# Factorization machine on one core: every load is issued by GpSimd instead of SP

## What is computed

```python
x_reg = x @ W_lin.T + b_lin
emb = x @ factors                                   # factors: 12500 x 16
sum_squared = square(emb.sum(axis=1))
squared_sum = (square(x) @ square(factors)).sum(axis=1)
h = relu(emb @ W1.T + b1)                           # 128
h = relu(h @ W2.T + b2)                             # 64
dnn_out = h @ W3.T + b3
y = x_reg + 0.5 * (sum_squared - squared_sum)[:, None] + dnn_out
y = 0.5 + sigmoid(y) * 5.0
```

## Time and profile before

| | |
|---|---|
| median of 3 runs | 133.75 us |
| the profiled execution | 133.76 us |
| its span, first to last instruction | 132.0 us |
| busy: PE / ACT / DVE / POOL | 81% / 47% / 40% / 12% of the span |
| moved by DMA | 52.36 MB, mean 397 GB/s |
| mean granted TensorE clock | 0.974 |
| chain that ended last | DMA 54%, PE 40%, SP's issues 2% |

### The profile page before, as it was taken

How to read it: one execution, slowest core, us unless ns; L and a number is a source line. 1 busy time by engine, 2 the same in 40 slices (tenths; PEclk the granted TensorE clock), 3 DMA queues, 4 the chain that set the end, 5 groups by cost and what they waited for, 6 DMA issues and landing times.

```text
span 132.0 us, 2607 instructions
## 1 busy us (share of the span) xinstructions
PE 107.0 (81%) x1123; PEld 34.6 (26%) x1123; DVE 52.6 (40%) x51; ACT 61.5 (47%) x52; POOL 15.7 (12%) x48
## 2 busy tenths in 40 slices
PE   6099969429979839749749979999998987989992
PEld 4012222002212112112112233322222112345881
DVE  0391063027036036046045016565351351576571
ACT  4030067029039039049048046868562561465851
POOL 3015000200010200200200110164530000000000
PEclk9999999995999999999977999999999999999999
DMA  3999899989999998998999999899999999999700
GB/s 106 413 531 417 377 477 472 407 387 467 427 387 462 457 427 387 457 437 387 467 457 427 387 457 447 377 432 412 452 407 407 462 415 417 418 404 411 302 26 1
DMA packets 3489, 52.36 MB, mean 397 GB/s; under 512 B 404, under 2 KB 536, under 8 KB 1560
## 3 DMA queue, kind: packets, MB, share of 16 engines
q1 hardware_dynamic: 3480, 52.23, 93.2%
HBM read 52.22 MB, written 0.00 MB: 396 GB/s over the span
## 4 chain that ended last, share of the span: by engine, by line
DMA 54%; PE 40%; SPq 2%; DVE 1%; issue 1%; ACT 1%
DMA xr<-in_x_pairs 43%; PE p_lin L506 34%; DMA xr<-in_x_end 11%; PE p_sq L506 2%; PE p_h L601 2%; SPq L273 1%; PE p_tot L506 1%; PE p_h L632 1%; PE p_tot L614 0%; DVE h L454 0%; DVE h L449 0%; SPq L267 0%; SPq L266 0%; PE p_tot L621 0%; SPq L265 0%
## 5 line engine op out<-in xcount | busy, mean ns | idle before, releaser
L327 ACT ACTIVATE sq<-xr 128x2560 f32<-128x2560 f32 x20 | 45.9, 2333 | 46.8 <-DMA xr<-in_x_pairs 38.8
L427 DVE TENSOR_TENSOR sq<-xr 128x1536 f32<-128x1536 f32 x20 | 34.6, 1761 | 53.7 <-DMA xr<-in_x_pairs 42.9
L506 PE MATMUL p_lin<-xr,wr 128*17 128x512 f32 x320 | 39.9, 638 | 15.6 <-DMA xr<-in_x_pairs 14.4
L506 PE MATMUL p_lin<-sq,wz 128*18 128x512 f32 x320 | 37.7, 592 | 0.0
L506 PEld LDWEIGHTS p_lin<-xr,wr 128*17 128x17 f32 x320 | 9.2, 102 | 44.5 <-issue 38.4
L307 POOL COPY wr<-hd 128x136 f32 (+1 forms) x20 | 9.3, 464 | 75.0 <-PE p_lin L506 75.0
L506 PEld LDWEIGHTS p_lin<-sq,wz 128*18 128x18 f32 x320 | 10.1, 98 | 25.8 <-issue 25.0
L506 PE MATMUL p_lin<-xr,hd 128*17 128x352 f32 (+1 forms) x128 | 10.0, 380 | 1.3 <-DMA xr<-in_x_end 1.3
L437 DVE TENSOR_TENSOR sq<-xr 128x1408 f32<-128x1408 f32 (+3 forms) x6 | 6.6, 1135 | 6.1 <-DMA xr<-in_x_end 6.1
L337 ACT ACTIVATE sq<-xr 128x1408 f32<-128x1408 f32 (+3 forms) x6 | 5.7, 983 | 6.3 <-DMA xr<-in_x_end 6.3
L506 PE MATMUL p_lin<-sq,ws 128*18 128x352 f32 x64 | 6.6, 459 | 0.0
(11 more groups left out here) (52 smaller groups left out, 40.8 us busy)
## 6 DMA issues: line engine op xcount, KB each, us to landing
xr<-in_x_pairs SPq DMA_DIRECT2D x8, 4096.0 KB, 21.9
xr<-in_x_groups SPq DMA_DIRECT2D x4, 2048.0 KB, 18.3
xr<-in_x_end SPq DMA_DIRECT2D x1, 2112.0 KB, 10.5
xr<-in_x_end SPq DMA_DIRECT2D x3, 640.0 KB, 12.0
xr<-in_x_end SPq DMA_DIRECT2D x1, 1760.0 KB, 14.3
xr<-in_x_end SPq DMA_DIRECT2D x1, 1056.0 KB, 12.4
hd<-in_head SPq DMA_DIRECT2D x1, 952.0 KB, 4.8
xr<-in_x_end SPq DMA_DIRECT2D x1, 704.0 KB, 13.7
```

Of the source, the lines that this page charges most:

```text
L327: nc.scalar.activation(sq[:, ring(s), BY_DVE:CHUNKS, :], xr[:, s, BY_DVE:CHUNKS, :], ACT.Square).then_inc(act_squared, 1)
L427: nc.vector.tensor_tensor(sq[:, ring(s), 0:BY_DVE, :], xr[:, s, 0:BY_DVE, :], xr[:, s, 0:BY_DVE, :], ALU.mult).then_inc(dve_squared, 1)
L506: return nc.tensor.matmul(out, lhsT, rhs, start=False, stop=False, skip_group_check=True)
```

## The change

All loads move from SP to GpSimd. SP keeps only the three stores of y. GpSimd issues head, x_first, x_rest and pairs 0 to 2 first, then zeroes the pads, and from then on its loads and its copies stand in one program, in the order of the `sq_used` counts that they wait for; of a load and a copy with the same count the load comes first. The hardware loop over 12 groups is written out. The copy of the end weights (`ws`, 32 columns) goes behind the copies for groups 0 to 2. The wait of an end piece loses END_SLOT: pieces 0 and 1 now wait for a count of 19 (before 21), pieces 2 and 3 for 20 (22), the others for 21 (23). Nothing changes on the other engines.

```diff
         @block.sync
         def _(sp):
-            sp.dma_start(hd[:, :], head).then_inc(hd_landed, 16)
-            sp.dma_start(xf[:, :], x_first).then_inc(first_landed, 16)
-            sp.dma_start(xl[:, :, :].rearrange("p c b -> p (c b)"), x_rest).then_inc(rest_landed, 16)
-            for p in range(PAIRED // TWO):
...
-                sp.wait_ge(sq_used, RING + TOTAL - SLOTS + END_SLOT + last_slot(i) + 1)
-                sp.dma_start(piece(i, c, n), rows).then_inc(end_landed[i], 16)
-                at += P * n * width(i)
-
             for k in range(len(BLOCKS)):
                 sp.wait_ge(y_ready[k], 1)
...
         @block.gpsimd
         def _(pool):
+            def load_pair(p):
+                at = TWO * p % SLOTS
+                if TWO * p >= SLOTS:
+
+                    pool.wait_ge(sq_used, RING + TWO * p + TWO - SLOTS)
+                nc.gpsimd.dma_start(xr[:, at:at + TWO].rearrange("p s c b -> p (s c b)"),
+                                    x_pairs[p, :, 0:TWO * CHUNKS * HALF]).then_inc(x_landed[at // TWO], 16)
+
+            def load_single(g):
+                pool.wait_ge(sq_used, RING + g + 1 - SLOTS)
+                nc.gpsimd.dma_start(xr[:, g % SLOTS].rearrange("p c b -> p (c b)"),
+                                    x_groups[g - PAIRED, :, 0:CHUNKS * HALF]).then_inc(single_landed[g - PAIRED], 16)
+
+            def load_piece(i):
+                c, n = PIECES[i][1], chunks(i)
+                at = sum(P * chunks(q) * width(q) for q in range(i))
+                rows = x_end[at:at + P * n * width(i)].rearrange("(p m) -> p m", p=P)
+                pool.wait_ge(sq_used, RING + TOTAL - SLOTS + last_slot(i) + 1)
+                nc.gpsimd.dma_start(piece(i, c, n), rows).then_inc(end_landed[i], 16)
+
+            nc.gpsimd.dma_start(hd[:, :], head).then_inc(hd_landed, 16)
+            nc.gpsimd.dma_start(xf[:, :], x_first).then_inc(first_landed, 16)
+            nc.gpsimd.dma_start(xl[:, :, :].rearrange("p c b -> p (c b)"), x_rest).then_inc(rest_landed, 16)
+            for p in range(SLOTS // TWO):
+                load_pair(p)
+
             nc.gpsimd.memset(wz[:, :, :, :], 0.0).then_inc(pads_set, 1)
             nc.gpsimd.memset(ws[:, :, :], 0.0).then_inc(pads_set, 1)
...
-            with pool.Fori(0, GROUPS // RING) as r:
-                for s in range(RING):
-                    place(RING * r + s, s, 1 + CHUNKS * (RING * r + s))
-            for g in range(GROUPS, TOTAL):
-                place(g, g, 1 + CHUNKS * (g - GROUPS))
...
+            place(0)
+            place(1)
+            place(2)
+            end_weights()
+            place(3)
+            for g in range(4, PAIRED - 3):
+                if g % TWO == 0:
+                    load_pair(g // TWO + 1)
+                place(g)
+            for g in range(PAIRED - 3, TOTAL - 3):
+                load_single(g + 3)
+                place(g)
+            place(TOTAL - 3)
+            load_piece(0)
+            load_piece(1)
+            place(TOTAL - 2)
+            load_piece(2)
+            load_piece(3)
+            place(TOTAL - 1)
+            for i in range(4, len(PIECES)):
+                load_piece(i)
```

More of the change, by code:

```diff
@@ L300, in _, with end_weights, place @@
             nc.gpsimd.tensor_copy(ws[:, 0, LIN:WZ], s_all[:, 0:1]).then_inc(ws_ready, 1)
-            nc.gpsimd.tensor_copy(ws[:, 1:ENDS + 1, LIN:WZ].rearrange("p c k -> p (c k)"),
-                                  s_all[:, W_END:ALL]).then_inc(ws_ready, 1)
-            def place(g, s, at):
-                pool.wait_ge(sq_used, g + 1)
-                nc.gpsimd.tensor_copy(wr[:, ring(s), :, :], w[:, bass.ds(at, CHUNKS), :]).then_inc(wr_ready, 1)
-                nc.gpsimd.tensor_copy(wz[:, ring(s), :, LIN:WZ].rearrange("p c k -> p (c k)"),
-                                      s_all[:, bass.ds(at, CHUNKS)]).then_inc(wz_ready, 1)
-            with pool.Fori(0, GROUPS // RING) as r:
-                for s in range(RING):
-                    place(RING * r + s, s, 1 + CHUNKS * (RING * r + s))
-            for g in range(GROUPS, TOTAL):
-                place(g, g, 1 + CHUNKS * (g - GROUPS))
+            def end_weights():
+                nc.gpsimd.tensor_copy(ws[:, 1:ENDS + 1, LIN:WZ].rearrange("p c k -> p (c k)"),
+                                      s_all[:, W_END:ALL]).then_inc(ws_ready, 1)
+            def place(g):
+                at = 1 + CHUNKS * (g % GROUPS)
+                pool.wait_ge(sq_used, g + 1)
+                nc.gpsimd.tensor_copy(wr[:, ring(g), :, :], w[:, at:at + CHUNKS, :]).then_inc(wr_ready, 1)
+                nc.gpsimd.tensor_copy(wz[:, ring(g), :, LIN:WZ].rearrange("p c k -> p (c k)"),
+                                      s_all[:, at:at + CHUNKS]).then_inc(wz_ready, 1)
+            place(0)
[19 more added lines that the diff above has]
+                load_piece(i)
         @block.scalar
```

## The result

The changed kernel took 134.70 us (median of 4 runs, 134.63 to 134.77), the kernel before 133.72 us beside it (4 runs, 133.61 to 133.87): a ratio of 1.0069 with a 95% interval of 1.0057 to 1.0082. It is 0.98 us slower, and 134.7 us was the forecast. The span went from 132.0 to 132.9 us.

A forecast was written before the change was run, and what follows sets the result against it. The prediction took one full, in-order DMA queue of loads as the bound, then PE work after end piece 1. 133.76 us plus 0.89 for the later first issue, all else 0, gave 134.65, so 134.7 us; range 133.3 to 136.6.

The forecast's parts named there:

- The first issue, +0.89 us: Start of the span: GpSimd's issue of the head takes 1.28 us against SP's 0.39, adding 0.89 us.
- price of 6 us for a first call: In the cold-first-issue rival (chance 0.05): a freshly loaded library kernel's first call costs about 6 us, giving 139.8 us or more.
- The delay is paid in full: First transfer: its later start, 0.89 us, moves the end of the span by the same amount.
- Every landing 0.9 us later: Sign in the timeline: the head's first use and every later landing shift by the same 0.9 us, steps kept.
- Rate and turnaround unchanged: Load queue: 2.300 us per MB and 0.073 us for each transfer (its turnaround) stay as they were.
- The pads: Start: zeroing behind six issues ends at 9.5 us, before DVE needs it; cost 0 unless an issue exceeds 1.4 us.
- the copies behind the issues: GpSimd's place copies come one issue late; tightest at group 15, with 3.4 us for issue and copy; cost 0.
- the earlier pieces: End pieces 0 and 1, issued 7 us earlier by lower counts, gain nothing, since the queue is in order and full.
- 11 us of cover: Singles issued from 85.38 us on: landing 16.3 us or more after issue, for 4.90 us of data, leaves 11 us.
- 5.4 us: Cover of the first end piece: it lands 10.5 us after its issue, for 5.05 us of data.
- late by one or two us reaches nobody: Loads in steady state: a GpSimd issue one or two us late costs nothing, since the least cover is 5.4 us.
- The clock rival: Tail, PE work after piece 1: PE's granted clock falls, losing 1.7 us, giving 136.4 us; chance 0.02.

The follow-up runs named there:

- memsets_first: The changed kernel with GpSimd's two pad memsets put back ahead of its first load: 135.14 us, ratio 1.0096 to the kernel before.
- split_pairs: The changed kernel with each 4096 KB pair loaded by two transfers of 2048 KB, eight transfers more: 135.36 us, ratio 1.0114 to the kernel before.
- head_by_sp: The changed kernel, but SP issues the head and GpSimd all loads behind it: 134.03 us, ratio 1.0012 to the kernel before.
- two_by_sp: The changed kernel, but SP issues head and x_first, GpSimd x_rest and all loads behind it: 133.86 us, ratio 1.0010 to the kernel before.
- old_waits: The changed kernel with the end pieces behind all copies and at their old counts (21, 22, 23): 134.64 us, ratio 1.0070 to the kernel before.
- pairs_one_later: The changed kernel with pairs 3 to 7 issued one group later (count higher by 1): 138.79 us, ratio 1.040 to the kernel before.
- early_pieces: The kernel before with the changed kernel's counts for the end pieces, issued by SP: 133.74 us, ratio 0.9996 to the kernel before.

## Why the prediction was right, point by point

- **The first issue, +0.89 us: right in size, partly by luck.** The prediction let GpSimd begin at 0.73 us and took one row, a table load of 1.28 us, for the length of the issue. In the trace the issue begins 0.51 us late and then takes only 0.67 us; from 0.73 us to its end that is 1.19 us. The issue ends 0.79 us later than SP's, and the head's landing came 0.90 us later. What fills the 0.5 us before GpSimd's first issue no run shows; memsets_first shows only that other work of GpSimd's can stand in it. The Trainium skill on the first byte ("DMA: Bandwidth & Descriptors", section "Latency and other measured facts") would have given +0.4 us. From the start of the issue to the landing seen the trace agrees, 4.80 us for SP and 5.19 for GpSimd, 0.39 more (0.25 to 0.59 more in the other kernels in which GpSimd issues the head, at the upper end in split_pairs); what is missing in that sum is the later start. The Trainium skill's price of 6 us for a first call ("GPSIMD Engine Reference", section "2.1 Instruction dispatch") was not seen: the first issue takes 0.14 us more than the second.
- **The delay is paid in full: shown** by memsets_first (the issue 0.47 us later, the time 0.35 to 0.51 us longer), by head_by_sp, which gave 0.7 to 0.8 us back, and by two_by_sp, which gave back all but 0.1 us (0 to 0.3 by its interval).
- **Every landing 0.9 us later: not quite.** From pair 1 to piece 1 the landings came 0.73 to 0.78 us later, and another 0.13 us came with piece 2, which was not foreseen. Only together do they give the 0.9 us of the span.
- **Rate and turnaround unchanged: right.** 430 GB/s, steps of 9.7 and 1.58 us, and 0.07 to 0.08 us for a transfer by split_pairs.
- **The pads, the copies behind the issues, the earlier pieces: cost 0, right.** With issues of 0.53 us nothing came near its limit, both edits to the pieces' counts measured nothing, and two_by_sp has all of these moves and loses nothing that could be told.
- **The cover was overstated.** The step that failed is "11 us of cover" for the singles and "5.4 us" for the first piece: both count to the landing. By the reading of pair 3 above some 3 us have to come off, and another 1.1 us for the time from an issue to its first bytes. That leaves, as an estimate, 7 us and 1.3 us. GpSimd's issues were later than SP's by about 0.5 us (0.29 us from TensorE's last product to the start of the issue against 0.02, and 0.53 us of issue against 0.33), so the sum did not feel it. For the same reason "late by one or two us reaches nobody" had less room than stated: old_waits, with the old counts, shows it for this half microsecond only.
- **The clock rival** found no support: no slice of the last 40 us has a granted clock below nine tenths, before or after. The changed kernel's mean granted clock was 0.961 in two of its runs and 0.985 and 0.987 in the others, at 134.67 and 134.63 against 134.77 and 134.73 us. It does act where an issue depends on TensorE with no cover left, as in pairs_one_later.

Open: the step from piece 1 to piece 2 is 2.69 us in the changed kernel and 2.56 before. In the other profiles it is between 2.55 and 2.85 us, 2.63 in early_pieces, where SP issues all loads, and 2.56 in memsets_first, where GpSimd does. So it goes with neither issuer; what moves it is not known. Open too are the 0 to 0.3 us that stay in head_by_sp. No version tried was faster than the kernel before by more than the measurement tells.

## What to carry to other kernels

In this kernel, which is bound by a full, ordered queue of loads, the start of the first transfer, the bytes and the number of transfers made the time; who issued the rest did not matter, as long as each issue came early enough. In a kernel like it, put the first issue on the engine that is quickest with it, and count cover to when the bytes run out and not to the landing: here issues under 3 us before the last queued landing always cost something, and one 5 us before it cost nothing. Do not put a small load that everything waits for on a second queue beside large rows: it gets one row for each large row.

## What was not expected

- Two queues take turns row by row, whatever the rows' size: a load of 384 KB landed at 23.7 us, with each of its 3 KB rows waiting for one of 32 KB.
- Nearly all bytes of the queue (14.36 of 14.47 MB) had moved 3 us before the last landing was seen, and issues 2.3 to 2.8 us before a landing lost anything from 0.34 to 2.09 us.
- GpSimd's first issue has 0.5 us ahead of it that a memset can fill; a later issue takes 0.53 us against 0.33 to 0.45 on SP.
